# Key features from three stacks of 128 rows, key norms moved by vector copies and added as the bias of one exponential per head

## The reference, cut to what matters

```python
def feature_map(x, orf):
    proj = x @ orf.T / d_k ** 0.25
    norm = jnp.sum(x * x, axis=-1, keepdims=True) / (2.0 * math.sqrt(d_k))
    return (jnp.exp(proj - norm) + EPS) / math.sqrt(m)
q = feature_map(split(x @ Wq.T + bq), orf)
k = feature_map(split(x @ Wk.T + bk), orf)
v = split(x @ Wv.T + bv)
kv = jnp.einsum('nlm,nld->nmd', k, v)
ksum = jnp.sum(k, axis=1)
out = jnp.einsum('nlm,nmd->nld', q, jnp.concatenate([kv, ksum[..., None]], axis=-1))
out = out[..., :-1] / out[..., -1:]
...
x = _layernorm(x + attention(x))
x = _layernorm(x + x @ (ternary(weight) * scale).T)
```

## Time and profile before

| | |
|---|---|
| median of 3 runs | 1302.82 us (1302.79 to 1304.18) |
| span of the profiled execution | 1300.4 us |
| PE busy | 1280.2 us, 98% |
| PE weight load busy | 965.9 us, 74% |
| DVE busy | 942.1 us, 72% |
| ACT busy | 702.1 us, 54% |
| POOL busy | 384.1 us, 30% |
| granted TensorE clock, mean | 0.998 |

### The profile page before, as it was taken

The page is one execution under the profiler, slowest core; times in us unless marked ns, Lnnn a source line. Parts: engine busy times, 40 slices in busy tenths (PEclk is TensorE's granted clock), DMA queues, the critical chain, the costliest instruction groups (busy, mean ns, idle before and its releaser), DMA issues.

```text
span 1300.4 us, 24924 instructions
## 1 busy us (share of the span) xinstructions
PE 1280.2 (98%) x8626; PEld 965.9 (74%) x8626; DVE 942.1 (72%) x1784; ACT 702.1 (54%) x1403; POOL 384.1 (30%) x685
## 2 busy tenths in 40 slices
PE   9999999999999999999999999999999999999987
PEld 8767787777877678776787768876788767887665
DVE  7599765886668875787657786587875787657876
ACT  5557435564355743657336663367534665446534
POOL 1213432125311343214421234312352123422143
PEclk9999999999999999999999999999999999999999
DMA  7668414773146821567215762258612686026711
GB/s 242 140 136 217 95 50 111 170 190 84 57 118 160 200 68 54 133 159 189 62 57 130 182 165 69 62 130 197 162 45 71 142 209 149 30 80 147 163 51 65
DMA packets 83773, 160.56 MB, mean 123 GB/s; under 512 B 19648, under 2 KB 37184, under 8 KB 83136
## 3 DMA queue, kind: packets, MB, share of 16 engines
q1 hardware_dynamic: 67856, 139.78, 43.4%
q10 hardware_dynamic: 9648, 16.85, 3.4%
q0 software_dynamic: 6144, 2.34, 2.1%
HBM read 39.13 MB, written 16.78 MB: 43 GB/s over the span
## 4 chain that ended last, share of the span: by engine, by line
PE 84%; DVE 6%; ACT 6%; issue 3%; DMA 1%; POOL 0%; SPq 0%; ACTq 0%; DVEq 0%; POOLq 0%
PE ps L943 28%; PE ps L980 25%; PE ps L1044 8%; PE ps L1012 4%; PE ps L966 4%; PE ps L968 4%; PE ps L967 4%; PE ps L999 4%; ACT features L687 2%; PE ps L1070 2%; ACT x_hi L655 1%; DMA rows<-in_Wk_t 1%; DVE squares_turned L853 1%; ACT unit_hi L668 0%; DVE cols L857 0%
## 5 line engine op out<-in xcount | busy, mean ns | idle before, releaser
L687 ACT ACTIVATE features<-ps 128x512 f32<-128x512 f32 x512 | 279.0, 603 | 254.4 <-PE ps L943 196.0
L584 POOL DMA_DIRECT2D stacks<-norm_rows x128 | 86.3, 681 | 305.7 <-DVE norm_rows L868 185.8
L943 PE MATMUL ps<-Wo_hi,stacks 128*128 128x512 f32 x448 | 150.4, 402 | 0.0
L660 ACT ACTIVATE values_then_attention<-ps 128x512 f32<-128x512 f32 x64 | 38.3, 598 | 197.2 <-PE ps L968 194.1
L809 DVE TENSOR_TENSOR den<-den,features 128x512 f32<-128x512 f32 x186 | 128.0, 688 | 12.7
L562 POOL TENSOR_SCALAR stats<-stats 128x1 f32<-128x1 f32 x128 | 36.1, 282 | 323.4 <-DVE stats L796 323.2
L943 PE MATMUL ps<-orf_key_a,stacks 128*128 128x256 f32 x512 | 131.4, 288 | 0.1
L943 PE MATMUL ps<-orf_key_b,stacks 68*128 68x256 f32 x512 | 128.2, 282 | 0.0
L1044 PE MATMUL ps<-features,kv_ksum 128*32 128x512 f32 x1024 | 123.1, 598 | 3.4 <-ACT features L687 2.1
L845 DVE SCALAR_TENSOR_TENSOR unit_lo<-ps,cols,unit_hi 128x512 fp32r<-128x512 f32 x128 | 94.2, 736 | 35.0 <-ACT squares L670 34.9
L943 PEld LDWEIGHTS ps<-orf_key_a,stacks 128*128 128x128 f32 x512 | 97.1, 190 | 25.9 <-issue 22.1
(11 more groups left out here) (141 smaller groups left out, 2773.2 us busy)
## 6 DMA issues: line engine op xcount, KB each, us to landing
stacks<-unit_hi SPq DMA_DIRECT2D x384, 128.0 KB, 2.4
stacks<-unit_lo SPq DMA_DIRECT2D x256, 128.0 KB, 3.7
stacks<-unit_hi SPq DMA_DIRECT2D x64, 256.0 KB, 3.9
out<-rows ACTq DMA_DIRECT2D x56, 256.0 KB, 2.0
rows<-in_x_t SPq DMA_DIRECT2D x49, 256.0 KB, 4.5
rows<-in_x SPq DMA_DIRECT2D x32, 256.0 KB, 4.3
features<-in_x SPq DMA_DIRECT2D x32, 256.0 KB, 4.2
values_then_attention<-in_x_t SPq DMA_DIRECT2D x8, 256.0 KB, 7.1
```

The source lines that it names most:

```text
L584: pool.dma_start(slot[row:row + 2, c:c + L].rearrange("o (t c) -> o t c", c=DH), NN[2 * DH * p:2 * DH * (p + 1), u % 2, part, :].bitcast(F ...
L687: nc.scalar.activation(FE[:, n % 8, :, 0:M], ps[:, :].rearrange("p (a m) -> p a m", a=HG), ACT.Exp, scale=C_EXP).then_inc(a_exp.sem, 1)
L943: last = mm(out, a, b, start=(n == 0), stop=(n == len(terms) - 1))
```

## The change

For keys a token tile's four heads need 4 x 96 = 384 rows (hi, lo and hi again of each head). Before, they lay in four column blocks: two with 128 rows (hi and lo of two heads, `orf_key_a`) and two with 68 rows (hi of two heads, and 4 rows with norms, `orf_key_b`), and a stage took four matmuls of 256 columns. After, they lie in three blocks of 128 rows, and a stage takes three matmuls of 256 columns that overlap in their output by a head. There are no norm rows for keys any more: the squares are scaled fully, DVE's sum is written negated as `key_norms`, and in N 16 DVE copies of 32 partitions x 8 elements bring head h's norms to the partitions of the tokens (`key_bias`). The exponential of a key stage becomes four, one a head, 128 columns each, with a column of `key_bias` as bias. Keys' NL falls away (four DMAs a unit), LIFT of keys issues 9 DMAs instead of 10. Queries stay as they were.

```diff
@@ ACT, stage F
-                    nc.scalar.activation(FE[:, n % 8, :, 0:M], ps[:, :].rearrange("p (a m) -> p a m", a=HG),
-                                         ACT.Exp, scale=C_EXP).then_inc(a_exp.sem, 1)
+                    if is_key(u):
+                        if r == 0:
+                            act.wait_ge(v_kn.sem, v_kn.nth(b, u // 2 + 1))
+                        for h in range(HG):
+                            last = nc.scalar.activation(FE[:, n % 8, h, 0:M], ps[:, M * h:M * (h + 1)], ACT.Exp,
+                                                        bias=NB[:, u // 2 % 2, h, r:r + 1], scale=C_EXP)
+                        last.then_inc(a_exp.sem, 1)
+                    else:
+                        nc.scalar.activation(FE[:, n % 8, :, 0:M], ps[:, :].rearrange("p (a m) -> p a m", a=HG),
+                                             ACT.Exp, scale=C_EXP).then_inc(a_exp.sem, 1)
@@ DVE, stages Q and N
-                    nc.vector.reduce_sum(NSUM[:, 16 * h:16 * (h + 1)], TQ[:, :].rearrange("p (a c) -> p a c", c=DH),
-                                         axis=mybir.AxisListType.X).then_inc(v_ns.sem, 1)
+                    blocks = TQ[:, :].rearrange("p (a c) -> p a c", c=DH)
+                    if is_key(u):
+                        if h == 0:
+                            dve.wait_ge(v_kn.sem, v_kn.nth(b, u // 2))
+                        by_tile = KN[:, :, 4 * h:4 * (h + 1)].rearrange("p a t -> p t a")
+                        nc.vector.reduce_sum(by_tile, blocks.rearrange("p (t a) c -> p t a c", a=4),
+                                             axis=mybir.AxisListType.X, negate=True).then_inc(v_ns.sem, 1)
...
+                elif kind == "N" and is_key(u):
+                    dve.wait_ge(v_ns.sem, v_ns.nth(b, 2 * u + 2))
+                    if b or u >= 4:
+                        dve.wait_ge(a_exp.sem, a_exp.nth(b, 8 * (u - 3)))
+                    for h in range(HG):
+                        for a in range(4):
+                            last = nc.vector.tensor_copy(NB[DH * a:DH * (a + 1), u // 2 % 2, h, :], KN[DH * h:DH * (h + 1), a, :])
+                    last.then_inc(v_kn.sem, 1)
@@ PE, stage F
-                        norms_lifted(pe, b, u)
-                    slot = ST[:, u % 2, :]
+                        if not is_key(u):
+                            norms_lifted(pe, b, u)
                     if is_key(u):
-                        for p in range(2):
-                            at_a, at_b = L * p + P * r, L * (2 + p) + P * r
-                            last = products(ps[:, 256 * p:256 * (p + 1)], [(slot[:, at_a:at_a + P], MA[:, :]),
-                                                                          (slot[0:KK, at_b:at_b + P], MB[0:KK, p, :])])
+                        for n in range(3):
+                            last = mm(ps[:, M * n:M * (n + 2)], KST[:, L * n + P * r:L * n + P * (r + 1)], MK[:, n, :],
+                                      start=(n == 0), stop=(n == 2), skip_group_check=True)
```

More of the change, by code:

```diff
@@ L274, in attention_kernel @@
         TQ, NT = sb("squares_turned", [P, HALF]), sb("norms_turned", [P, DH])
-        NN = sb("norm_rows", [P, 2, 2, DH], F32R)
+        NN = sb("norm_rows", [P, 2, DH], F32R)
+        KN, NB = sb("key_norms", [P, 4, TT]), sb("key_bias", [P, 2, HG, TT])
         DR = sb("den", [P, 2, HALF])
@@ L578, in lift_norms @@
                     wait(t_ff.sem, t_ff.nth(b, 0))
-                wait(v_n.sem, v_n.nth(b, 3 * u + 3))
+                wait(v_n.sem, v_n.nth(b, 3 * (u // 2) + 3))
                 for part in range(2):
-                    if is_key(u):
-                        for p in range(2):
-                            row, c = 2 * DH + 2 * part, L * (2 + p)
-                            pool.dma_start(slot[row:row + 2, c:c + L].rearrange("o (t c) -> o t c", c=DH),
-                                           NN[2 * DH * p:2 * DH * (p + 1), u % 2, part, :].bitcast(F32))\
-                                .then_inc(n_lifted[0].sem, 16)
-                    else:
-                        row = 3 * DH + part
-                        pool.dma_start(slot[row:row + 1, :].rearrange("o (t c) -> o t c", c=DH),
-                                       NN[:, u % 2, part, :].bitcast(F32)).then_inc(n_lifted[1].sem, 16)
+                    row = 3 * DH + part
+                    pool.dma_start(slot[row:row + 1, :].rearrange("o (t c) -> o t c", c=DH),
+                                   NN[:, part, :].bitcast(F32)).then_inc(n_lifted.sem, 16)
             for kind, b, at, _, _ in steps():
                 t = at[0] if at else 0
-                if kind == "NL":
+                if kind == "NL" and not is_key(t):
                     lift_norms(b, t)
@@ L629, in split_hi @@
                     act.wait_ge(t_o.sem, t_o.nth(b, t - 1))
-                nc.scalar.activation(ST[:, 1, D * (t % 2):D * (t % 2 + 1)], VA[:, t, :], ACT.Copy).then_inc(a_ahi.sem, 1)
+                nc.scalar.activation(QST[:, D * (t % 2):D * (t % 2 + 1)], VA[:, t, :], ACT.Copy).then_inc(a_ahi.sem, 1)
             def apply_norm(k, b, t):
@@ L763, in constant_rows @@
                     nc.vector.tensor_tensor(WQS[r, h, :], wT[r, 0:M], rounded[r, :].bitcast(F32), ALU.subtract)
[L764 to L771 removed]
+                for n, q, a in ((0, 2, 0), (1, 1, 0), (2, 0, 0), (2, 3, 1)):
+                    r = slice(DH * q, DH * (q + 1))
+                    nc.vector.tensor_tensor(MK[r, n, M * a:M * (a + 1)], wT[r, 0:M], rounded[r, :].bitcast(F32), ALU.subtract)
+                nc.vector.tensor_copy(WQS[3 * DH:QK, :, :], minus_one).then_inc(s_orf, 1)
             def weight_scale():
@@ L998, in _ @@
                         c = L * h + HALF * half
-                        last = mm(ps[:, :], WQS[0:QK, h, :], slot[0:QK, c:c + HALF], start=True, stop=True)
+                        last = mm(ps[:, :], WQS[0:QK, h, :], QST[0:QK, c:c + HALF], start=True, stop=True)
                     last.then_inc(t_f.sem, 1)
```

99 lines of the change are left out of this document (44 added, 55 removed).

## The result

The changed kernel takes 1342.48 us (median of 4 runs, 1339.35 to 1346.37), the kernel before beside it 1303.19: ratio 1.0301, 95% interval 1.0282 to 1.032. It is 3% slower; the prediction was 1300.9. The profiled execution is the slowest of the four (1346.37, span 1344.5), 44.1 above the span of before.

A forecast was written before the change was run, and what follows sets the result against it. PE bounds the kernel, with 84% of the chain. -30.7 (PE) + 20.0 + 3.8 (ACT) + 2.4 + 2.6 (DVE, batch 0) = -1.9 us against the 1300.4 span: 1298.5, as a median 1300.9; range 1289 to 1312.

The forecast's parts named there:

- Key matmuls of 256 columns start 0.12 us apart: On PE, one matmul less in each of 8 stages: 0.96 us a key unit, 30.7 in 32 units.
- ACT's pitch: On ACT in key stages: 128-column exponentials start 0.25 us apart, between bounds of 0.17 and 0.36.
- the second rival: Key exponentials on ACT have a pitch of 0.29 us, about 12 us more: 1313; chance 0.15.
- the first (ACT not late): Rival: ACT is not late in unit 0, 20.0 and most of 3.8 come back: about 1279; chance 0.23.
- What ACT pays: Longer key stages on ACT make PE late: 20.0 us in unit 0 over 8 batches, 3.8 in the last unit 6.
- Bounds are 0.07 and 0.17 each, 1.2 and 2.7 us together; I take 1.2, since the copies don't depend on each other.: On DVE in a key unit's N: 16 copies take 1.2 us, so N is 0.6 longer.
- N over 1.5 us: Sign in the profile, on DVE in key units, that would show the prediction wrong.
- The third rival: DVE's copies in N don't overlap, N is 1.4 us longer yet, about 10 us in all: 1311; chance 0.10.
- The keys' NL and one of LIFT's DMAs fall away, but PE never waited for either: On the DMAs of key units: removing them changes nothing in the time.
- what costs nothing: Step listing parts without effect on time: the negated sum, the removed DMAs, ACT's wait for the copies.
- PE's gain: On PE, one matmul less a key stage: 30.7 us over 32 key units if nothing else is late.
- The forecast's DVE part: Longer N delays the copy for GG in unit 7 of six batches, 2.4 us; batch 0 and setup, 2.6.

The follow-up runs named there:

- the square: Four kernels: the changed one (1342.5 us), with one copy for 16 (1314.4), with one exponential for four (1317.9), with both edits (1286.0).
- a: The changed kernel with N's 16 DVE copies replaced by one copy of 128x32, norms at wrong places: 1314.4 us.
- c: The changed kernel with one copy in N and one 512-column exponential without bias a key stage, key norms left out: 1286.0 us.
- n: The changed kernel with 16 DVE copies all from partitions 0 to 31 to 32 to 63, key norms left out: 1317.0 us.
- j: The changed kernel with eight unread matmuls of 512 columns added in PE's wait ahead of GG in unit 7 of seven batches: 1335.4 us.
- h: c with POOL waiting, where it issued the keys' norm DMAs before, until the unit's squares are summed: 1277.5 us.
- l: The changed kernel, whole, with POOL's x additions of each batch's first two tiles waiting for DVE's copy of the turned result: 1330.5 us.

## Why the prediction was wrong, by its steps

*Held.* "Key matmuls of 256 columns start 0.12 us apart", one less a stage: three in each stage at that distance, units 2 and 4 won 0.97 and 0.85. ACT's pitch, "I take 0.25, its own kind": 0.25 in the row, so the second rival (0.29) is out, and the first (ACT not late) too, unit 0 being 24.37. "What ACT pays", 20.0 + 3.8: the square gives 28.4, as 7 x 2.67 in units 0 (forecast 2.5), 4.9 in the last unit 6 (3.8) and 4.8 in batch 0 (2.5). The mechanism was right, the size 5 short, half of it in batch 0, where the profiled executions of a and c differ in the clock too (0.83 and 1.00 from 61 to 71 us). In the changed kernel the four activations of the ternary weight are followed there by a matmul that PE waits 2.9 for, and the clock is 0.57 for the next 7.30 us, a window of the changed kernel:

```profile
64.70:72.00 7.30, 7.29 (x56) 5.80 (x57) 3.39 (x20) 4.52 (x14) 0.00 (x0) 0.57 0.34 80
```

*The step that failed.* "Bounds are 0.07 and 0.17 each, 1.2 and 2.7 us together; I take 1.2, since the copies don't depend on each other." They take 2.80, just over the upper bound, and the prediction's own sign of being wrong, "N over 1.5 us", is there. The range of the price was right and the choice in it wrong: overlap needed not only independence but the same partition group as the copy before (n). That alone is 25.5 us between n and the changed kernel. The third rival had the right mechanism and a tenth of the chance, and its price, "1.4 in six batches and in batch 0, about 10", was far too small. It counted N's additional length once. The stretch paid 3.1 a batch between n and the changed kernel for 1.55 us more of N: about 1.7 for GG's later start, and the rest for GG and what follows at a lower clock in five of seven batches (j gives back 7.1 us). Unit 4, batch 0 and the last batch pay on top.

*The step that was missed.* "The keys' NL and one of LIFT's DMAs fall away, but PE never waited for either", under what costs nothing. PE didn't; POOL did. Without those DMAs in its queue the x additions ran in unit 6, against DVE's feature additions: 8.4 us from h to c, 12.0 from l to the changed kernel. Whose start a removed instruction held back was never asked.

*PE's gain* was 25.3 (h against before), not 30.7: in h unit 0 wins 0.74 and the stretch 0.75 instead of 0.96, the stretch from the last unit 6 to the end only 0.10, and batch 0's units 2 and 4 0.24 and 0.27. For these last the prediction had taken 0.96 and 1.9 out again, in its terms for ACT and DVE; why unit 0 and the stretch give less than 0.96 isn't shown.

So the sum, in medians: 1302.8, -25.3 for the third stack (h), +8.4 for POOL's early additions (c), +28.4 for the exponentials (a), +28.1 for the copies: 1342.5. The forecast's DVE part was 5.0 of the last, and had nothing for the second.

## What to carry to other kernels

A price between two bounds is settled by the condition under which each bound was measured: the row for 0.07 stayed in one partition group, the change's copies don't, and the casts of the setup showed both cases. When an instruction is taken out of a queue, list what stands behind it there and what that will now run beside. And a wait of PE can cost more than its length: behind 2.1 us of it the granted clock fell in five of seven batches, for 2.0 us each.

## What the runs showed of the hardware

- 16 DVE copies of 32x8 start 0.073 us apart if all read one group of 32 partitions and write one other, and 0.176 apart if the group written changes each time; each lasts 0.15 to 0.17.
- POOL's copies of 32x8, one behind the other by a semaphore, are 0.25 apart ((3.87 - 0.18) / 15).
- A DVE copy of 0.16 us took 3.49 beside POOL's DMA issues and additions, and a pair of DVE additions 2.80 instead of 1.49 beside POOL's additions, which took 3.11 instead of 2.55.
- Behind a wait of PE of 2.11 to 2.14 us the granted clock fell in five of seven batches of one execution, and GG's 16 matmuls took 2.67 to 3.59 us instead of 1.92; PE was about equally busy in a window with the fall and in one without (4.39 and 4.36 of 6.50 us).
- Eight matmuls with no use, put into a wait of PE, made the kernel 7.1 us faster (1342.5 to 1335.4); the clock fell in none of the seven.
